# Cross attention regrouped: steps of eight chunks, and transposes, scores, products in that order

## What is computed

```python
a = jnp.einsum('bqd,bkd->bqk', query, key)        # query = layernorm(x): (8, 64, 2048)
e = jax.nn.softmax(a, axis=-1)                    # key = ctx_4096: (8, 1601, 2048)
c = jnp.einsum('bqk,bkd->bqd', e, key)
x = x + c                                         # then attention and feed-forward
```

## Time and profile before

| | |
|---|---|
| median of 3 runs | 1657.05 us (1655.38 to 1658.23) |
| the profiled execution | 1651.15 us, of which the span from first to last instruction is 1649.4 |
| TensorE busy | 1622.6 us, 98% of the span |
| VectorE, ScalarE, GpSimd busy | 783.4, 554.1, 473.6 us |
| cross attention | from 0 to about 600 us of the span |

### The profile page before, as it was taken

One profiled execution on the slowest core, in us unless ns is written; L12 is line 12 of the kernel. 1 busy time (PEld: TensorE's weight loads), 2 busy tenths in 40 slices (PEclk: granted clock), 3 DMA queues, 4 the chain that ended last, 5 costly groups with the idle time before them and its releaser, 6 DMA issues.

```text
span 1649.4 us, 22682 instructions
## 1 busy us (share of the span) xinstructions
PE 1622.6 (98%) x8929; PEld 1201.6 (73%) x8929; DVE 783.4 (47%) x1336; ACT 554.1 (34%) x790; POOL 473.6 (29%) x161
## 2 busy tenths in 40 slices
PE   6999999999999999999999999999999999999999
PEld 5565555555556558888888888888888888887877
DVE  3454646455464460164364545543644450248323
ACT  2433334343434332232332333323323323222221
POOL 0000000000011003356466465564663663440010
PEclk9999999999999999999999999999999999999999
DMA  9566666666767534223333233233233342220023
GB/s 312 183 207 205 207 207 217 200 225 195 232 213 238 178 104 153 77 77 103 102 102 93 85 102 102 76 102 102 78 100 102 102 153 77 83 99 24 26 77 128
DMA packets 178888, 224.58 MB, mean 136 GB/s; under 512 B 4240, under 2 KB 102544, under 8 KB 176048
## 3 DMA queue, kind: packets, MB, share of 16 engines
q1 hardware_dynamic: 178816, 223.56, 42.4%
HBM read 212.54 MB, written 11.01 MB: 136 GB/s over the span
## 4 chain that ended last, share of the span: by engine, by line
PE 97%; DVE 1%; ACT 1%; DMA 1%; issue 0%; SPq 0%; DVEq 0%; ACTq 0%
PE ps L817 14%; PE ps L819 14%; PE ps L818 14%; PE ps L683 12%; PE ps L750 11%; PE ps L724 10%; PE ps L1858 5%; PE ps L1857 5%; PE ps L1856 5%; PE ps L1796 2%; PE ps L1949 1%; PE ps L1821 1%; PE ps L695 1%; DMA xa_raw_a<-in_ctx 1%; PE ps L1805 0%; PE ps L728 0%
## 5 line engine op out<-in xcount | busy, mean ns | idle before, releaser
L817 PE MATMUL ps<-h_hi,w_hi 128*128 128x512 f32 x800 | 315.4, 394 | 1.2 <-DVE h_lo L1513 1.1
L819 PE MATMUL ps<-h_hi,w_lo 128*128 128x512 f32 x800 | 311.6, 390 | 0.0
L818 PE MATMUL ps<-h_lo,w_hi 128*128 128x512 f32 x800 | 311.5, 389 | 0.0
L1245 POOL TENSOR_TENSOR w_lo<-raw,w_hi 128x2048 fp32r<-128x2048 f32 (+1 forms) x52 | 212.8, 4095 | 329.3 <-ACT w_hi L1310 288.1
L452 ACT ACTIVATE xa_ct<-ps 128x512 f32<-128x512 f32 x256 | 152.8, 598 | 185.0 <-PE ps L683 113.9
L628 DVE COPY xa_ct<-ps 128x321 f32<-128x321 f32 (+1 forms) x256 | 117.4, 459 | 201.6 <-PE ps L683 126.8
L724 PE MATMUL ps<-xa_ct,xa_q_t 128*64 128x384 f32 x1024 | 183.6, 488 | 0.0
L817 PEld LDWEIGHTS ps<-h_hi,w_hi 128*128 128x128 f32 x800 | 150.2, 188 | 36.5 <-issue 6.5
L819 PEld LDWEIGHTS ps<-h_hi,w_lo 128*128 128x128 f32 x800 | 150.2, 188 | 31.7
L818 PEld LDWEIGHTS ps<-h_lo,w_hi 128*128 128x128 f32 x800 | 150.3, 188 | 29.9
L1601 DVE TENSOR_TENSOR rows<-rows,ps 128x512 f32<-128x512 f32 x168 | 115.5, 688 | 116.1 <-PE ps L1858 116.1
(11 more groups left out here) (245 smaller groups left out, 2327.1 us busy)
## 6 DMA issues: line engine op xcount, KB each, us to landing
xa_raw_a<-in_ctx SPq DMA_DIRECT2D x32, 1536.0 KB
xa_raw_b<-in_ctx SPq DMA_DIRECT2D x32, 1536.0 KB, 6.7
raw<-in_L_attn_w_q SPq DMA_DIRECT2D x32, 1024.0 KB, 5.8
raw<-in_L_attn_w_o SPq DMA_DIRECT2D x30, 1024.0 KB, 5.0
raw<-in_L_attn_w_k SPq DMA_DIRECT2D x8, 1024.0 KB, 5.8
raw<-in_L_attn_w_v SPq DMA_DIRECT2D x8, 1024.0 KB, 5.8
xa_xq<-in_x SPq DMA_DIRECT2D x8, 512.0 KB, 5.2
xa_raw_a<-in_ctx SPq DMA_DIRECT2D x32, 128.0 KB
```

Source lines behind the costliest of these rows:

```text
L817: pe.matmul(out, hi, mov_hi, start=first, stop=False)
L818: pe.matmul(out, hi, mov_lo, start=False, stop=False)
L819: return pe.matmul(out, lo, mov_hi, start=False, stop=last)
L1245: pool.tensor_tensor(w_lo[:, n % 2, part], raw[:, n % 2, part], w_hi[:, n % 2, part].bitcast(F32), ALU.subtract).then_inc(w_lo_done, 1)
```

## The change

- `CHUNKS` is 8 and `PER` 2: a step holds eight chunks, there are 32 steps. The two PSUM places stay two. `xa_ct` holds four chunks as before; the second four get `xa_ct_late`, which lies where the scratch of the DMA descriptors was (16 KB, now 2 KB).
- On TensorE a step is now T of eight chunks, S of the same eight, then V of the stage before (six or seven uses: two column groups).
- The exponentials are needed one step earlier (`PV_AT` 0 for 1): the softmax of a stage is made at the end of its last step, behind its scores, while the products run.
- The layernorm for the next batch stands in one piece behind the copies of the first step of a batch (`NORM_AT = 0`), for batch 1 behind those of step 0. SP issues the query load for the batches from 2 on in the last step of a batch, instead of at the start of the next.
- `groups_now` and `groups_late` say when VectorE and ScalarE empty a column group: the even one in its own step, the odd one behind the copies of the next.
- `first_queries` (the transposes of the queries of batch 0, L707) come behind the eight chunks of step 0 instead of two; the ScalarE copy of them too.
- The weight loads and splits stand at steps 25, 27 and 26, 28 (before 50, 53 and 52, 55).

The core of the diff:

```diff
-CHUNKS, UNITS = 4, 2
+CHUNKS, UNITS = 8, 2
+PIECE = 4
-PV_AT = 1
+PV_AT = 0
...
+def groups_now(t):
+
+    return [(h, c) for h, c in groups_before(t, 0) if h == STAGES - 1 or c % 2 == 0]
+
+
+def groups_late(t):
+
+    return [(h, c) for h, c in groups_before(t, 1) if h < STAGES - 1 and c % 2]
...
-STATS_AT, CHAIN_AT, NORM_AT = (2, 3, 4, 5), (5, 6), 6
+NORM_AT = 0
...
-WEIGHT_LOAD_AT, WEIGHT_SPLIT_AT = (50, 53), (52, 55)
+WEIGHT_LOAD_AT, WEIGHT_SPLIT_AT = (25, 27), (26, 28)
...
+    here[0] = LATE_KEYS_AT
+    ct_late = sb("xa_ct_late", [P, CHUNKS - PIECE, KEYS[0] + 1])
...
+            b, at = divmod(t, HALVES * PER)
+            if at == Q_AT and b + 2 < B:
+                sp.wait_ge(t_done, chunk_no(t, CHUNKS - 1) + 1)
+                load_rows(b + 2, xq, xq_in)
...
+            if b < B - 1 and at == NORM_AT:
+                dve.wait_ge(xq_in, 16 * (b + 2))
+                for c in range(NCOL):
+                    row_stats(c)
+                some(layernorm_links(), 11)
+                for c in range(NCOL):
+                    normalize(c)
+            if t < STEPS and i == PER - 1:
+                maxima(t // PER)
...
-                if t == 0 and u == UNITS - 1:
+                if t == 0 and u == CHUNKS - 1:
                     first_queries()
+            if t < STEPS:
+                scores(t)
             for h, n in USE_AT.get(t, []):
                 product(h, n)
-            if t < STEPS:
-                scores(t)
...
-    nc = _bacc.Bacc("TRN2", target_bir_lowering=False, num_devices=1)
+    nc = _bacc.Bacc("TRN2", target_bir_lowering=False, num_devices=1, dynamic_dma_scratch_size=SCRATCH)
```

More of the change, by code:

```diff
@@ L117, in side_transposes @@
     for b in range(1, B):
-        for u in range(CHUNKS):
-            at[HALVES * PER * (b - 1) + Q_AT, u] = [("q", b, 4 * u + k) for k in range(4)]
+        for u in range(DC // 4):
+            at[HALVES * PER * (b - 1) + Q_AT, CHUNKS - DC // 4 + u] = [("q", b, 4 * u + k) for k in range(4)]
     return at
@@ L445, in exponentials, with softmax, group_out @@
                 act.activation(sum_low[:], row_sum[LQ:P, :], ACT.Copy).then_inc(sums_ready, 1)
+        def softmax(h):
+            x = h % HALVES
+            if x == 0:
+                both(act, s_done, h + 1)
+                act.activation(odd_half[:], ps_s[LQ:P, h % 2, MAIN:MAIN + ODD], ACT.Copy).then_inc(odd_copied, 1)
+            act.wait_ge(max_done, h + 1)
+            act.activation(mx_low[:, x:x + 1], mx[LQ:P, x:x + 1], ACT.Copy).then_inc(max_low, 1)
+            act.wait_ge(neg_ready, h + 1)
+            act.activation(neg_max[LQ:P, x:x + 1], neg_max[0:LQ, x:x + 1], ACT.Copy).then_inc(stats_ready, 1)
+            exponentials(h)
+        def group_out(gh, c):
+            b, x = divmod(gh, HALVES)
+            if x == 0 and b == B - 1:
+                both(act, pv_done, group_over(gh, c))
+                if c < 2:
+                    act.wait_ge(folded, NCOL * b)
+                else:
+                    act.wait_ge(first_out, NCOL * b + c - 1)
+                act.activation(low[:, c % 2, :], group_bank(gh, c)[LQ:P, :], ACT.Copy).then_inc(first_low, 1)
+            elif x == 0:
+                both(act, pv_done, group_over(gh, c))
+                act.activation(acc[:, column(c)], group_bank(gh, c), ACT.Copy).then_inc(first_out, 1)
+            else:
+                if b < B - 1:
+                    act.wait_ge(rescaled, NCOL * b + c + 1)
+                else:
+                    both(act, pv_done, group_over(gh, c))
+                    if c < 2:
+                        act.wait_ge(first_out, NCOL * B)
+                    else:
+                        act.wait_ge(finished, NCOL * b + c - 1)
+                act.activation(low[:, c % 2, :], group_bank(gh, c)[LQ:P, :], ACT.Copy).then_inc(low_ready, 1)
         for t in range(ALL_STEPS):
-            h, i = t // PER - 1, t % PER
+            i = t % PER
             if t < STEPS:
@@ L451, in cross_scalar @@
                     act.wait_ge(t_done, chunk_no(t, u) + 1)
[L452 to L485, removed]
@@ L631, in cross_vector @@
                 ins.then_inc(second_copied, 1)
-            if i == 0 and 0 <= h < STAGES:
-                maxima(h)
-            if i == 1 and h > 0 and h % HALVES == 1:
+            if i == 0 and 0 < h < STAGES and h % HALVES == 1:
                 row_total(h // HALVES)
+            if t == E_LAST:
+                first_fold(NCOL - 1)
+            for gh, c in groups_late(t):
+                group_in(gh, c)
             for gh, c in groups_before(t, 1):
@@ L642, in cross_vector @@
                                   ALU.mult, ALU.mult).then_inc(out_stats, 1)
[L643 to L661, removed]
+            if b < B - 1 and at == NORM_AT:
[5 more added lines that the diff above has]
+                    normalize(c)
+            if t < STEPS and i == PER - 1:
+                maxima(t // PER)
+            for gh, c in groups_now(t):
+                if gh == STAGES - 1:
                     for n in ((0, 1), (2,), (3,), ())[c]:
```

83 lines of the change are left out of this document (49 added, 34 removed).

## The result

The changed kernel takes **1662.64 us** (median of 11 runs, 1657.73 to 1666.16), the kernel before 1658.05 us in the runs beside it (1655.38 to 1658.46). The ratio is 1.0027, 95% interval 1.0017 to 1.0038: slower by 0.27%, or 4.6 us. The profiled execution took 1662.03 us, with a span of 1660.2.

A forecast was written before the change was run, and what follows sets the result against it. TensorE was taken as the bound, 97% of the chain that ended last. Terms -10, +6.7, 0, +0.3, +6.7, +1.8 and +1.6 sum to +7.1 us, which on 1657.05 gives 1664.2 us, 0.43% slower; range 1658.5 to 1671.

The forecast's parts named there:

- part 1: Entering and leaving T (the transposes) 32 times instead of 64 saves 0.33 us each time: 10 us gained.
- part 2: In a T of eight chunks three pairs in four wait for copies, before one in two: 6.7 us lost.
- part 3: Softmax one step earlier, behind a stage's last scores: hidden by six or seven uses of V and transposes, nothing lost.
- part 4: Layernorm in one piece, steady part: VectorE has 0.3 us slack; with the second split, 0.3 us lost in all.
- Part 5: Same layernorm in step 0: queries land at 29.4 us, TensorE stands still 7.3 us, stage 0 ends 6.7 us later.
- Part 6: Behind that stillness TensorE transposes at half pace: three chunks cost 0.6 us more each, 1.8 us in all.
- part 7: First weight split on ScalarE delays the copy of the first chunk of the next T: 1.6 us lost.
- at that price: Chunks with side transposes stream and copy longer; their added waits stay at 0.27 us (six transposes) or 0.15 (seven).
- the 5.3 that was named as a sign: In the changed trace, S between T and V of half 1 takes under 5.3 us.
- the rival with 7 us more: VectorE is late by 0.5 us in two steps of each of seven batches: +7 us, 1671 us; chance 15%.
- Parts 7 and 8: The first split's 1.6 us lost, and the loads: pieces land in time for their reading, nothing lost.
- The carry-over to the median: The +7.1 us worked out on the profiled execution (1651.15 us) is added to the median 1657.05: 1664.2 us.

The follow-up runs named there:

- tiny copies: ScalarE copies 128 of 512 keys, VectorE 64 of 256 or 321: in the kernel before 1640.5 us, in the changed kernel with layernorm and both splits moved 1635.56 us.

## Why the prediction was right, and where it was not

The time, 1662.64 us, lies within the range and 1.6 us from 1664.2, and the sign is right. The number is in part luck, as the last point below says. Term by term, in the two profiled executions and, for parts 1 and 2, with the tiny copies:

| term | predicted | measured | how |
|---|---|---|---|
| part 1, changes of form | -10 | -8.14 | tiny copies, above |
| part 2, waits for copies | +6.7 | +5.73 | (555.11 - 537.56) - (557.85 - 545.70 - 0.33) |
| part 3, softmax | 0 | +2.28 | T of step 2: 8.95 against 6.67 later |
| part 4, layernorm and second split | +0.3 | +0.07 | T of step 29: 6.52 against 6.45 |
| parts 5 and 6, start | +8.5 | +6.77 | stage 0: 36.31 us against 29.54 |
| part 7, first split | +1.6 | +1.24 | 1.57 (T of step 27: 9.47 against 7.90) less 0.33 |
| sum | +7.1 | +7.95 | 7.94 by the starts |

555.11 is stage 1 to the end of the changed kernel, 559.03, less 2.28, 1.57 and 0.07. The 0.33 is what the same split cost before (T of step 53: 3.91 against 3.58).

- **Parts 1 and 2** had the mechanism right and both sizes too large; the net, -2.4 against -3.3, is the right sign and not far off. What part 2 has too much lies in the T's with side transposes, which the prediction left "at that price". In the first T of a half 1 the added wait is 0.07 us and not 0.27, in eight stages 1.6 us less; in the first T of a half 0 it is 0.27 and not 0.15, in seven stages 0.8 more. S of eight chunks takes 5.21 us in half 1 (56.10 to 61.31), under the 5.3 that was named as a sign. The Trainium skill, "TensorEngine Tiling (Array Packing)", section Key Properties, names the drain at a change of mode and no price; these runs agree with it, at 0.27 us for one T less.
- **Part 3 failed.** "Nothing" was argued from six or seven uses of V behind the last scores of a stage. Stage 0 has none: nothing precedes it, so behind its scores the transposes of step 2 follow at once. The row stands above: L728 waits 2.06 us for L449. I had checked the steady case and not the first stage.
- **Part 4**: VectorE is late in no batch; the rival with 7 us more fell.
- **Part 5**: the mechanism held, row by row (the DMA ahead of L534, the copy L665 behind L544). Its size hung on the landing: the queries came at 26.8 us and not at 29.4, and the stillness was 5.26 us and not 7.3. Less the 0.6 that the prediction takes off its own 7.3, and with the 2.1 of part 6, that is the measured 6.8. The order of the loads was a fair guide all the same: issued 2.7 us later than before, the queries did not land later. What differed was how fast the keys ahead of them moved in the execution at hand. 29.4 was the latest landing of all twelve executions; the one of this trace was among the early ones.
- **Part 6** held in its result: half pace, 2.1 us (6.98 against 4.87) for a predicted 1.8. Its ground was thinner than it looked: the second execution of before is at half pace behind the same gap of 1.8 us at which the first was at full pace.
- **Parts 7 and 8** held: 1.24 us for the split over what it cost before, and no wait for a piece of keys in the changed kernel.
- **The carry-over to the median** was the weak step, and errors cancelled in it. I took the profile of before as typical but for 5.9 us. Its stage 0 lacked a stretch of half pace that three later executions with the same start have (stage 0 over at 42.67, 42.86 and 43.23 instead of 40.84), the two kernels with shortened copies among them. Against the second execution of before, cross attention got 5.2 us longer (595.34 against 590.15), near the 4.6 of the timed runs. So of the 7.9 us of the trace pair some 3 are the clock's and not the change's. The missing softmax (2.3 us too little) and the start and clock taken too large go opposite ways: forecast for the medians were 7.1 us, measured 4.6, from a base that came out 1.0 higher (1658.05 for 1657.05). The profiled execution itself was forecast at 1658.3 and took 1662.03, 3.4 of it by the decoder.

What stays open: the softmax of stage 0. Copies of the first chunks ahead of it on ScalarE and VectorE should hide it, some 2.3 us and half pace behind it at times. That is argued from the order of the engines and was not tried. Open is also whether the landing, from 26.1 to 29.4 us, is why the changed kernel scatters more (1657.73 to 1666.16 us, before 1655.38 to 1658.46); no run shows it.

## What to carry to other kernels

Making an engine's phases longer to save changes between them also takes away the pauses in which its helpers catch up: here 8.1 us saved brought 2.4. A rule that holds in the steady state must be read once more for the first stage, where the work that covers a wait may not exist, and for every load whose consumer moves ahead of its arrival. And work of another kind (a layernorm, a split) belongs where the work behind it has slack, not ahead of the next copies: moving the layernorm alone gave back 0.39% of the time. Moving the splits as well gave back 1.57 us in the trace, which the timed runs do not resolve (0.44% for all of it). Last, one profile against one profile misleads by some us here; a second execution of the kernel before showed which part of the difference was the clock's.

## What the runs showed of the hardware

- Half pace comes behind a gap in one execution and not in another. In the kernel before, the gap of 0.77 us in the decoder had it in the second execution and not in the first. Behind the 2.06 us of step 2 the clock stayed at 1.00 in the changed kernel and was 0.84 over that T with the layernorm moved. Such a stretch cost 1.4 us there, 2.1 us behind the stillness, and the two in the decoder of the changed kernel 3.4 us together (1054.05 against 1050.66). The Trainium skill, "TensorE: Matmul & The Clock Gate", Part 1, says of the start of a kernel that the number of slow products varies from run to run; the two executions of before agree (17.57 us: 1.47; 17.45 us: 2.74 for the same 14 loads).
- In both of these the granted clock of step 0 is given as 1.00 while the first transposes take nearly twice their time (2.75 and 2.74 us for 14 loads, 1.47 at full pace); there only the durations tell.
- A small load issued behind large ones landed when it did whether it was issued sooner or later, which fits that it waited for them. The 512 KB of queries landed at 26.7 to 29.4 us when issued at 16.6 to 17.9 (four executions with the order of before), and at 26.1 to 29.3 when issued at 19.9 to 21.2 (eight with the new order). The time from issue to landing, 11.5 or 6.2 us, says little by itself. The landing was latest where the keys ahead moved slowest from 11 to 17 us (332 GB/s: 29.4; 337: 29.3) and earliest where they moved fastest (390: 26.1).
- Half the keys did not halve a copy: ScalarE took 0.60 us for 512 keys, 0.38 for 256 and 0.28 for 128. T lost only 3.0 us of its 12.2 us of waits with ScalarE's copy halved, and all of them only when both engines' copies were cut.
